# Three small VectorE operations put in front of the output gate's pre-activation, and taken from GpSimd, ScalarE and the row's end

## The reference, cut to what matters

```python
h = _layernorm(x) * (1 + ca) + sa
normed = h * rsqrt(mean(h * h, -1) + EPS) * norm_w
q, k, v = normed @ Wq.T * scale, normed @ Wk.T * scale, normed @ Wv.T
zi, zf = normed @ wi_w[0] + wi_b[0], normed @ wf_w[0] + wf_b[0]
o = sigmoid(normed @ Wo.T + bo)
# scan over the tokens:
m_t = maximum(zf_t + m, zi_t)
C_t = exp(zf_t + m - m_t) * C + exp(zi_t - m_t) * outer(v_t, k_t)
n_t = exp(zf_t + m - m_t) * n + exp(zi_t - m_t) * k_t
h_t = o_t * (C_t @ q_t) / maximum(abs(sum(n_t * q_t)), 1)
x = x + ga * (h + h_t @ Wout.T)
# then: layernorm, modulation, 8 experts of 128 -> 256 -> 128, the two best by the router, x + gb * y
```

## Time and profile before

| | us |
|---|---|
| median of 3 runs | 331.12 |
| the runs | 327.93, 331.12, 331.92 |
| the profiled execution | 327.37 |
| its span, first to last instruction | 325.6 |
| TensorE busy in the span | 314.3 (97%) |
| VectorE busy | 264.2 (81%) |
| GpSimd busy | 171.5 (53%) |
| ScalarE busy | 166.0 (51%) |

### The profile page before, as it was taken

One profiled execution on the slowest core, in us unless ns is written; L12 is line 12 of the kernel. 1 busy time (PEld: TensorE's weight loads), 2 busy tenths in 40 slices (PEclk: granted clock), 3 DMA queues, 4 the chain that ended last, 5 costly groups with the idle time before them and its releaser, 6 DMA issues.

```text
span 325.6 us, 5182 instructions
## 1 busy us (share of the span) xinstructions
PE 314.3 (97%) x1775; PEld 257.9 (79%) x1775; DVE 264.2 (81%) x801; ACT 166.0 (51%) x311; POOL 171.5 (53%) x181
## 2 busy tenths in 40 slices
PE   8989989999999999999999999999999999999996
PEld 7778856888887878787788888787888778777995
DVE  5786777998699886998599868987779859987875
ACT  1542525565637645464656473573555564346442
POOL 6450470388626964476538952596506762526440
PEclk9999999999999999999999999999999999999999
DMA  5870002300160007100530017000710034006101
GB/s 135 249 211 0 2 0 75 157 0 0 55 239 3 0 2 260 32 1 0 162 134 1 0 34 259 2 2 1 251 42 1 0 116 179 0 2 209 51 2 32
DMA packets 13456, 23.63 MB, mean 73 GB/s; under 512 B 1763, under 2 KB 8086, under 8 KB 12406
## 3 DMA queue, kind: packets, MB, share of 16 engines
q1 hardware_dynamic: 13202, 23.17, 22.1%
q10 hardware_dynamic: 164, 0.07, 0.1%
q0 software_dynamic: 64, 0.07, 0.1%
HBM read 21.07 MB, written 2.23 MB: 72 GB/s over the span
## 4 chain that ended last, share of the span: by engine, by line
PE 79%; DVE 8%; DMA 6%; ACT 2%; issue 2%; SPq 1%; POOL 1%; DVEq 0%; POOLq 0%
PE bank L1142 9%; PE bank L1144 8%; PE bank L1168 8%; PE bank L1158 8%; PE bank L1143 8%; PE bank L1159 8%; PE bank L1072 6%; DMA gate_bc<-gates_d 3%; PE bank L999 3%; PE bank L1187 2%; PE bank L1014 2%; PE bank L1019 2%; DMA br_bc<-in_L_ffn_br_dram 2%; PE bank L1193 1%; DMA gates_d<-gate_rows 1%
## 5 line engine op out<-in xcount | busy, mean ns | idle before, releaser
L482 POOL TENSOR_TENSOR hg_lo<-hg,hg_hi 128x512 fp32r<-128x512 f32 x65 | 87.4, 1356 | 66.5 <-ACT hg_hi L535 50.6
L876 DVE SCALAR_TENSOR_TENSOR hg<-bank,neg_b,gate_bc 128x512 f32<-128x512 f32 x128 | 94.3, 743 | 25.5 <-DMA gate_bc<-gates_d 13.2
L535 ACT ACTIVATE hg_hi<-hg 128x512 fp32r<-128x512 f32 x128 | 79.8, 629 | 62.2 <-DVE hg L876 60.8
L1142 PE MATMUL bank<-h_hi,w_hi 128*128 128x512 f32 x128 | 58.3, 456 | 1.5 <-ACT gate_rows L581 1.5
L1168 PE MATMUL bank<-hg_lo,w_hi 128*128 128x512 f32 (+1 forms) x144 | 53.2, 369 | 0.0
L1158 PE MATMUL bank<-hg_hi,w_hi 128*128 128x512 f32 (+1 forms) x144 | 53.1, 369 | 0.0
L1159 PE MATMUL bank<-hg_hi,w_lo 128*128 128x512 f32 (+1 forms) x144 | 52.9, 367 | 0.0
L1144 PE MATMUL bank<-h_lo,w_hi 128*128 128x512 f32 x128 | 50.4, 394 | 0.0
L1143 PE MATMUL bank<-h_hi,w_lo 128*128 128x512 f32 x128 | 50.3, 393 | 0.0
L889 DVE TENSOR_TENSOR hg_lo<-hg,hg_hi 128x512 fp32r<-128x512 f32 x63 | 48.0, 761 | 1.1 <-ACT hg_hi L535 0.6
L445 POOL TENSOR_SCALAR var_eps<-mv 128x4 f32<-128x4 f32 x16 | 4.0, 250 | 65.2 <-DVE mv L616 65.2
(11 more groups left out here) (175 smaller groups left out, 538.9 us busy)
## 6 DMA issues: line engine op xcount, KB each, us to landing
gate_bc<-gates_d SPq DMA_DIRECT2D x8, 1024.0 KB, 7.0
gate_bc<-gates_d SPq DMA_DIRECT2D x8, 512.0 KB, 4.9
gate_bc<-gates_d SPq DMA_DIRECT2D x14, 256.0 KB, 3.7
out_dram<-x_all SPq DMA_DIRECT2D x7, 256.0 KB, 2.3
w_raw<-in_L_ffn_W_dram SPq DMA_DIRECT2D x1, 1024.0 KB, 8.8
x_all<-in_L_attn_x_dram SPq DMA_DIRECT2D x2, 256.0 KB, 4.0
wmod_sb<-in_L_wmod_dram SPq DMA_DIRECT2D x1, 384.0 KB, 4.7
out_dram<-x_all SPq DMA_DIRECT2D x2, 128.0 KB, 1.9
```

The costliest lines, as they stand in the source:

```text
L482: g.tensor_tensor(hg_lo[k][:, :], hg[k][:, :], hg_hi[k][:, :].bitcast(fp32), ALU.subtract).then_inc(s_lo_pool, 1)
L535: a.activation(hg_hi[k][:, :], hg[k][:, :], ACT.Copy).then_inc(s_hghi, 1)
L876: v.scalar_tensor_tensor(hg[k][:, :], up_bank[n % 4][:, :], neg_b1[:, n:n + 1], gate_bc[own % 2][:, n // NU, :], ALU.max, ALU.mult).then_i ...
L1142: t_.matmul(dst, w_hi, hx, start=True, stop=False)
```

## The change

Three operations on 128x4 numbers move. The square `rms2` goes from GpSimd (t = 8) to VectorE (t = 9). The copy of `rms` into the column of `vs` goes from ScalarE (t = 10) to VectorE (t = 9). The reciprocal `rms_inv` goes from the end of the row to t = 9, on the same engine. The three stand behind VectorE's wait for `rms` and ahead of `zo`. The semaphores for the reciprocal and the column, and GpSimd's two waits ahead of the square, fall away.

```diff
@@ GpSimd
                     if t == 8 and start:
                         pool.wait_ge(s_mse, m2 + 1)
                         g.tensor_tensor(rms[:, :], ms_eps[:, :], minus_half[:, :], ALU.pow).then_inc(s_rms, 1)
-                        pool.wait_ge(s_rms, m2 + 1)
-                        if m2 > 0:
-                            pool.wait_ge(s_v, m2)
-                        g.tensor_tensor(rms2[:, :], rms[:, :], rms[:, :], ALU.mult).then_inc(s_rms2, 1)
@@ ScalarE
-                    if t == 10 and start:
-
-                        act.wait_ge(s_rms, m2 + 1)
-                        a.activation(vs[:, :, DH], rms[:, :], ACT.Copy).then_inc(s_vcol, 1)
@@ VectorE, middle(t)
                         if t == 9:
                             dve.wait_ge(s_rms, m2 + 1)
+                            v.tensor_tensor(rms2[:, :], rms[:, :], rms[:, :], ALU.mult).then_inc(s_rms2, 1)
+                            v.reciprocal(rms_inv[:, :], rms[:, :])
+                            v.tensor_copy(vs[:, :, DH], rms[:, :])
@@ VectorE, after the last step
-                    v.reciprocal(rms_inv[:, :], rms[:, :]).then_inc(s_rinv, 1)
-                    dve.wait_ge(s_rinv, m2 + 1)
                     dve.wait_ge(s_pv, m2 + 1)
@@ TensorE, t == 18
                         pe.wait_ge(s_P, m2 * NT + NT)
-                        pe.wait_ge(s_vcol, m2 + 1)
```

More of the change, by code:

```diff
@@ L250, in adaln_mlstm_moe_kernel @@
         s_rms2 = sem("s_rms2")
-        s_rinv = sem("s_rinv")
-        s_vcol = sem("s_vcol")
         s_vz = sem("s_vz")
```

## The result

The changed kernel takes 330.34 us (median of 20 runs, 329.55 to 332.62), the kernel before 328.58 us (20 runs, 326.61 to 333.75). The ratio is 1.007, with a 95% interval of 1.0047 to 1.0093: slower by some 2.3 us, which the 20 runs tell from no change, though it is under 2%. The two medians differ by 1.76 us only, since all ratios leave out slow runs (here six of the kernel before, over 1.5% above its fastest). I had forecast slower by 0.7 us. The span of the profiled execution goes from 325.6 to 328.0 us. The granted clock of single executions lies between 0.98 and 1.00, and what it costs falls mostly into the first two bodies: in the traces here with a granted clock of 1.00 from 40 to 62 us the second masked product comes 28.4 to 28.5 us behind the first, with 0.92 there 29.9 to 30.0 us, with 0.84 31.5 us.

What follows compares the result with a forecast made beforehand. TensorE was taken to bound the kernel, busy 210.9 of 213.0 us over the steady part. Six steady bodies (0.3) plus the first body (0.4) gave +0.7 us on 331.12: 331.8 us, range 328.0 to 334.1.

Steps and rivals of the forecast that it cites:

- the first, 0.3: Six steady bodies: a later `m_col` costs TensorE 0.05 us a body, 0.3 us in all, between 0 and 1.2.
- the second, 0.4: First body: copy or square hangs beside GpSimd's `xn`, `zo` 1.0 us later, price 0.4 us, between 0.1 and 1.0.
- The square hangs, `zo` 1.30 us late: VectorE, steady body: the square lasts until GpSimd's `hg_lo` of block 8 ends, so `zo` starts 1.30 us late, not 0.25.
- The copy hangs as well: VectorE in front of `zo`: a copy within SBUF also hangs beside GpSimd, and would hang in the square's place.
- Both gaps take back 1.24 us, 0.06 are left: VectorE, steady body: gaps ahead of `lg` (0.64 us) and the `hg` at 185.46 (0.60) absorb the 1.30 us delay but 0.06.
- the wait for `m_chunk`, forecast to stay: TensorE's weight load in a steady body: its wait stays at 0.5 us, the remaining 0.06 us vanishing.
- The path over GpSimd to `top_d`: Steady body: later `hg_hi` of block 10 moves the third `hg_lo`, `top_d` and `m_col` by 0.2 us; 0.0 to 0.2 come through.
- The removed work, price 0: GpSimd's square, ScalarE's copy, and the row-end reciprocal with its wait (0.20 us on VectorE) go: each gains 0.
- No hanging: First rival, in front of `zo`: square not blocked, `zo` 0.25 us later, 331.2 us; chance 0.22 with the hiding rival.
- The row's end: Second rival: 0.20 us removed between `hg` and `den` lets the next row go earlier in all eight, 329.5 us; chance 0.10.
- The second hang of the copy: Third rival: copy comes behind the start of `h2_lo`, hangs until 183.5, `zo` moves 3.3 us; +12.4, 343.5 us; chance 0.04.
- The fourth: Rival: TensorE's pace hides the whole change in each body, the first too, 331.1 us; chance 0.22 with the no-hanging rival.

Runs made afterwards that it cites:

- held kernel: Changed kernel, but GpSimd waits behind the power until VectorE's copy is done, and only then starts `hg_lo` of block 8; ratio 1.0014.
- scan and `top_d` moved out of the way: Changed kernel with the scan `zp` placed behind the two `vs` products and `top_d` behind the indices of the two best experts; ratio 1.0031.
- reciprocal alone: Kernel before, with only the reciprocal moved from the row's end to in front of `zo`, square and column left in place; ratio 0.9997.
- reciprocal and copy: Kernel before, with reciprocal and copy moved to VectorE in front of `zo`, and the square kept on GpSimd behind the power; ratio 1.0002.
- square from the reciprocal, ScalarE's copy: Changed kernel, but the square is made as VectorE's reciprocal of `ms_eps`, and the column of `vs` is copied on ScalarE again; ratio 0.9989.
- before, `top_d` behind: Kernel before, with `top_d` placed behind the indices of the two best experts; ratio 1.0007.
- reciprocal and copy, `top_d` behind: Kernel before, with reciprocal and copy in front of `zo`, square left on GpSimd, and `top_d` behind the indices; ratio 0.9994.

## Why the prediction was right in its sign and mis-sized

**The total: near by luck.** The 331.8 us were counted from a median of three runs, 331.12, which lies 2.5 us above that of 20, 328.58; from there +0.7 gives 329.3, and 330.34 was measured. Of the two terms of +0.7 the first, 0.3, measured over 2 us, and the second, 0.4, nothing.

**The square hangs, `zo` 1.30 us late: right.** Forecast 1.2 us in six bodies and an end 0.02 us behind `hg_lo`; measured 1.24 and 0.02. `zo` starts 1.33 us behind the power's end, 0.06 before: 1.27 late. The held kernel shows that it is GpSimd's start that does it.

**The copy hangs as well: right as a rule** (1156 ns when no square stands ahead of it), and in the changed kernel it didn't need to, as written.

**"Both gaps take back 1.24 us, 0.06 are left": this step failed.** I moved `zo`, `zg`, `zp` and `vs` together by 1.30 us and asked only whether TensorE would notice. I did not ask, as I had for the square, what stands beside each of them on GpSimd at its new time. The scan `zp` has two SBUF inputs, `ones` and `zg`. Before, it began at 181.69, just as `hg_lo` ended (181.75), and took 164 ns. 1.3 us later it meets `h2_lo`, and takes 0.60. VectorE is then 1.7 us late at the end of `vs`. The `hg` of t = 12 is still 0.30 us late (it starts 6.64 us behind the product of step 9, before 6.34), and this reaches `m_chunk` as 0.14. So the wait for `m_chunk`, forecast to stay, grew by 0.14 us. With the scan behind `vs` this `hg` starts at 6.33 again, and `m_chunk` is on time.

**The path over GpSimd to `top_d`: right in mechanism, wrong in size.** I had `hg_lo` of block 10 0.2 us late and the end of `top_d` with it. The scan's hang made it 0.6 us: its `hg` comes 1.7 us late and not 1.3. The pair now starts so late (186.53 for blocks 10 and 11) that `top_d` meets the second of them near its start and hangs for the rest of it: 1.16 us instead of 0.67, and `m_col` reaches TensorE 0.44 us late. The term "0.05 a body, 0.3 us in all, at most 1.2" measured 2.47 us, or 2.8 by the table. With scan and `top_d` moved out of the way, the term is what I had forecast for the square alone, near 0, in five of six bodies.

**The first body, +0.4: wrong.** It gave nothing. Between the power and `xn` stands GpSimd's small add. The square ran beside it in 164 ns, as with nothing in its way; the copy started 0.02 us behind `xn` by the records and took 141 ns all the same:

```profile
17.44 0.23 POOL L443 TENSOR_SCALAR var_eps<-mv 128x4 f32<-128x4 f32 x1
17.63 1.06 POOL L447 TENSOR_TENSOR xn<-x_all,mv 128x512 f32<-128x512 f32 x1
```

```profile
17.49 0.16 DVE L762 TENSOR_TENSOR rms<-rms 128x4 f32<-128x4 f32 x1 [0.51 <-POOL rms L462]
...
17.66 0.14 DVE L764 COPY vs<-rms 128x4 f32<-128x4 f32 x1
```

It looks like the kernel with GpSimd's square kept, where a short GpSimd operation in between let VectorE in. But there the copy started ahead of the long operation, and here, by 0.02 us, behind it; which of the two was really first such a small difference can't show, and no run settles why this copy didn't hang.

**The removed work, price 0: right as a gain, wrong as a loss.** The reciprocal at the row's end alone: 0.9997. ScalarE's copy and GpSimd's square: no gain anywhere, but the latter was the gate that kept `hg_lo` back.

**The rivals.** No hanging fell at the square's 1240 ns. The row's end fell with the reciprocal alone. The second hang of the copy didn't come, since it ran at 182.68, 0.7 us ahead of `h2_lo`, as worked out; but its form, a second hang further down the order, did come, with the scan in the copy's place. It was the right kind of rival, with the wrong operation, and a price of 0.4 and not 2.0 us a body because only the rest of `h2_lo` was left. The fourth, that TensorE's pace hides all, fell with the 0.47 us a body.

**What varies besides.** The total from the second to the last masked product differs by some 1.1 us among the kernels in which neither the square nor the copy hangs (212.65 us before). VectorE's wait for the DMA of `gate_bc` goes with it:

| kernel | wait for `gate_bc`, us | second to last masked product, us |
|---|---|---|
| reciprocal and copy | 12.2 | 211.70 |
| GpSimd held | 12.8 | 212.25 |
| square from the reciprocal, ScalarE's copy | 12.9 | 212.42 |
| before | 13.2 | 212.65 |
| reciprocal alone | 13.3 | 212.81 |
| before, `top_d` behind | 13.4 | 212.83 |
| reciprocal and copy, `top_d` behind | 13.4 | 212.85 |

The changed kernel has a wait of 12.8 us and 215.12 us, which is 2.87 more than the held kernel with the same wait: the six times 0.47 of the table. So the change itself costs 2.8 us in this trace, and a DMA wait that was shorter by 0.4 hid a part. Why this wait differs from kernel to kernel is not settled.

## What to carry to other kernels

In these traces an operation of 4 columns was not small when it had two SBUF inputs, or was a copy within SBUF, and GpSimd went on to a long one at the same moment: price it at the rest of GpSimd's running instruction. After such a delay, walk the whole order behind it again and set each such operation against GpSimd's timeline at its new time; the second hang may cost more than the first. The reciprocals (160 to 179 ns) and `zo`, which has one input in PSUM (some 0.27 us a tile beside a running `hg_lo`), did not hang anywhere here. A wait, or a short operation, on GpSimd ahead of its long one removed the hang at no cost that the runs can tell (1.0014 and 1.0002).

## What the runs showed of the hardware that I had not expected

- The scan with two SBUF inputs hangs like a two-input elementwise operation: 164 ns alone, up to 1217 ns behind an `hg_lo` that started 0.06 us ahead of it. The page "SBUF — State Buffer" of the Trainium skill, section "Who interferes with whom", speaks of instructions with two SBUF inputs; the trace agrees for the scan too.
- The one that waits gets in at the next boundary between two GpSimd instructions, even when GpSimd's next one is ready: the scan that ends at 184.74, with `h2_lo`, while the next `hg_lo` is recorded from 184.68. And a GpSimd instruction of 0.2 us ahead of the long one was enough to spare the copy its hang (175 against 1156 ns).
- The scan behind `vs` hung for 0.15 us in five bodies and for 1.05 us in the sixth, where it began 0.07 us behind an `hg_lo` instead of inside `h2_lo`: how late an operation comes decides which of GpSimd's it meets, and how much of that is left.
